# A second load of x in another order of tokens, tiles of neighbouring tokens, and stores per pair of tiles

## The chip, the cores and the metric

One core of a Trainium2 chip runs the kernel. The metric is the device time in microseconds of one execution, as the median of several runs. The engines named below are TensorE (PE; its weight loads are PEld), VectorE (DVE), ScalarE (ACT), GpSimd (POOL) and SyncE (SP); 16 DMA engines move data between HBM and SBUF.

## The reference

x has 4 sequences of 4096 tokens of 512 numbers in float32. Each token is normalised, and two branches are added to it:

```python
xn = _layernorm(x, axis=-1)
x = x + attention(xn) + ffn(xn)

def ffn(xn):                                   # M = 64, INNER = 16
    s = einsum('btd,dm->btm', xn, Win) + bin_
    h = relu(s[..., None] * W1 + b1)           # 16 values for each s
    g = einsum('btmh,mh->btm', h, W2) + b2
    return einsum('btm,md->btd', g, Wout) + bout
```

The attention's result is not zero for the first 16 tokens of a sequence alone (it indexes the token axis with the number of heads), so the kernel computes it once for 64 tokens, beside the main work. Nearly all of the work is the feed-forward branch over 16384 tokens.

## The kernel before

The tokens are taken in 16 **pairs** of blocks, 1024 tokens a pair, 512 a block (`h` or `b`, 0 and 1). A pair of x is 2 MB and lies in one of 6 ring buffers `x_sb`, 128 partitions x 4096 numbers. The kernel is a pipeline of 19 **bodies** (`BODIES = N + 3`): body n loads ahead, transposes pair n and forms s for it, scales and spreads s of pair n-1, takes ReLUs for pairs n-1 and n-2, sums them over the 16 inner values, and projects and adds pair n-3. Every engine has its instructions written out in a fixed order per body (`pe_program`, `act_program`, `dve_program`, `pool_program`, `sp_program`); the attention's instructions are put between them at places of a list (`AT_PE` and the like), up to body 8. Engines meet only by semaphores.

How s gets x with the 512 numbers of a token along the partitions:
- Block 0: PE transposes 128 x 128 pieces of `x_sb` (line 457) into PSUM, ACT copies them to `xT` (line 642).
- Block 1 (from pair 2 on, `n >= BY_PE`): the block is read from HBM **a second time**, into `xq`, such that VectorE's transpose of 32 x 32 squares (line 922) makes the whole turn. Here these are called **quads**. One half of the block, 256 tokens or 0.5 MB, is one `xq` buffer; there are three. Partition group i of 32 holds columns 128 i to 128 i + 127.
- `s_product` (line 478) then multiplies both with the centred Win, block 0 to partitions 0 to 63, block 1 to partitions 64 to 127.

VectorE takes the two transposes of a body (`turn_quads`) at its head and in its middle, between the four additions (`add`, line 912), the statistics of x (line 939), and the product and difference on s. PE's `project` (line 537) loads columns of G as weights and multiplies them with Wout; `add` adds its result to `x_sb` in place, and that is stored. An addition covers one tile of 128 tokens from each of both blocks.

All of these transfers are issued by SP, on one queue. Its order in a body n is: first half of the quads of pair n+1 (8 transfers), first store of pair n-3, both loads of pair n+2, second half of the quads of pair n+1 (8 transfers), second store of pair n-3:

```python
                if n > 2 and has(n + 1):
                    load_quads(2 * (n + 1 - BY_PE))
                if has(n - 3):
                    store(n - 3, 0)
                if n + AHEAD >= RING and has(n + AHEAD):
                    for h in range(2):
                        load(sp, n + AHEAD, h)
                if has(n + 1):
                    load_quads(2 * (n + 1 - BY_PE) + 1)
                if has(n - 3):
                    store(n - 3, 1)
```

A quad half waits until VectorE has turned the half that lay in its buffer, three halves earlier (`tq_done`). A load waits until the stores of the pair that lay in its ring buffer have landed (`st`). A store waits for two of the four additions (`add_done`).

Which token lies where: token p*4 + j of a block lies on partition p, tile j. A partition thus loads 8 KB in one run and stores 4 KB in one run. So that s has the tokens in their own order, PE's transposes write every fourth column of PSUM (`j::TILES`), and `project` reads every fourth column of G. A quad transfer covers 32 neighbouring tokens of all four column groups: 128 rows of 512 bytes, 64 KB.

Of the kernel before, what the change touches and what calls it, by code (L numbers as in the profile page):

```python
# [11 lines left out]
P = 128  # L12
RING = 6
# [7 lines left out]
def residual_block(nc, x, Wq, bq, Wk, Wv, bv, Wo, bo, lna_w, lnc_w, lnd_w, Wlq, blq, Wlk, blk, Wlv, blv,  # L21
# [6 lines left out]
    TPP = 8  # L28
    BLK = TPP // 2 * P
    PAIR = 2 * BLK  # L30
    N = B * T // PAIR
# [12 lines left out]
    NV = 5  # L44
    QH = BLK // QD // 2


    x_v = x.rearrange("b (n h p j) d -> (b n) h p (j d)", h=2, p=P, j=TPP // 2)
    out_v = out.rearrange("b (n h p j) d -> (b n) p h (j d)", h=2, p=P, j=TPP // 2)

    xq_v = x.rearrange("b (n h t a) (i d) -> (b n) h i a t d", h=2, t=BLK // QD, a=QD, d=P)
    pe, act, dve, pool, sp = nc.tensor, nc.scalar, nc.vector, nc.gpsimd, nc.sync
# [4 lines left out]
    with ctx:  # L57
# [14 lines left out]
        xT = sb("xT", [P, DC, BLK])  # L72
        xqT = sb("xqT", [P, BLK // QD, DC, QD])
        xT1 = xqT[:, :, :, :].rearrange("p t c a -> p (t c a)").rearrange("p (c n) -> p c n", c=DC)
        s_full = sb("s_full", [P, BLK])
# [74 lines left out]
        ldq = [sem(f"ldq{r}") for r in range(3)]  # L150
        st = [[sem(f"st{r}{h}") for h in range(2)] for r in range(RING)]
        tr_done, ev_done, tq_done, sc_done = sem("tr_done"), sem("ev_done"), sem("tq_done"), sem("sc_done")
# [61 lines left out]

        def by_part(t, i):

            return t.rearrange("p (h i d) -> p h i d", h=2, d=2 * D)[:, :, i, :]

        def out_part(n, i):
            return out_v[n, :, :, 2 * i * D:2 * (i + 1) * D]  # L220

        HALF = TPP // 2 * D


        def load(queue, n, h):

            m = n % RING
            if n == 3 and h == 0:
                queue.wait_ge(turned, 2 * DC)
            elif n == 4 and h == 0:  # L230
                queue.wait_ge(qk_ps, 1)
            elif n == 5 and h == 0:
                queue.wait_ge(turned, 4 * DC)
            elif n >= RING and h == 0:
                for i in range(2):
                    queue.wait_ge(st[m][i], 16 * (n // RING))
            queue.dma_start(x_sb[m][:, h * HALF:(h + 1) * HALF], x_v[n, h, :, :]).then_inc(ld[m][h], 16)  # L237

        def load_quads(k):

            r, n, h = k % 3, k // 2 + BY_PE, k % 2
            if k > 2:
                sp.wait_ge(tq_done, k - 2)
            for t in range(QH):
                sp.dma_start(xq[r][:, t * P:(t + 1) * P], xq_v[n, 1, :, :, h * QH + t, :]).then_inc(ldq[r], 16)  # L245

        def load_weight(i, w):
            sp.dma_start(w_nat[i], w.rearrange("(c p) i -> p c i", p=P)).then_inc(in_w[i], 16)

        def store(n, i):  # L250
            m = n % RING
            if n < N - 1:
                sp.wait_ge(add_done, TILES * n + 2 * (i + 1))
                sp.dma_start(out_part(n, i), by_part(x_sb[m][:, :], i)).then_inc(st[m][i], 16)  # L254
            else:
                for j in (2 * i, 2 * i + 1):
                    sp.wait_ge(add_done, TILES * n + j + 1)
                    sp.dma_start(out_v[n, :, :, j * D:(j + 1) * D], by_tile(x_sb[m][:, :], j)).then_inc(st[m][i], 16)

        def sp_program():  # L260
# [32 lines left out]
            for n in range(2, BODIES):  # L293
                if n > 2 and has(n + 1):
                    load_quads(2 * (n + 1 - BY_PE))
                if has(n - 3):
                    store(n - 3, 0)
                if n + AHEAD >= RING and has(n + AHEAD):
                    for h in range(2):
                        load(sp, n + AHEAD, h)  # L300
                if has(n + 1):
                    load_quads(2 * (n + 1 - BY_PE) + 1)
                if has(n - 3):
                    store(n - 3, 1)

# [139 lines left out]
        def transpose(n, part):  # L445

            m = n % RING
            for g in (2 * part, 2 * part + 1) if n < BY_PE else (part,):
                b, c = divmod(g, DC)
                if c == 0:  # L450
                    pe.wait_ge(ld[m][b], 16 * (n // RING + 1))
                free = groups(n) + g - (1 if n < BY_PE else 0)
                if free > 0:
                    pe.wait_ge(ev_done, free)
                for j in range(TILES):
                    col0 = b * HALF + j * D + c * P
                    mm = pe.transpose(bank(n, g)[:, j::TILES], x_sb[m][:, col0:col0 + P], ident[:, :])  # L457
                mm.then_inc(tr_done, 1)

        def s_product(n):  # L460
# [9 lines left out]
            for c in range(DC):  # L470
                for b in range(2):
                    if b == 0:
                        w, turned_x = win, xT[:, c, :]
                    elif n < BY_PE:
                        w, turned_x = win, xT1[:, c, :]
                    else:
                        w, turned_x = winq, xqT[:, :, c, :]
                    mm = pe.matmul(s_ps[b * M:(b + 1) * M, :], w[:, c, :], turned_x, start=(c == 0), stop=(c == DC - 1))  # L478
                mm.then_inc(sc_done, 1)

        def spread_rstd(n):
            pe.wait_ge(rstd_done, 2 * n + 2)
            if n > 1:
                pe.wait_ge(g_made, n - 1)
            for j in range(TILES):
                mm = pe.transpose(g_ps[:, j::TILES], rwide[:, j, :, :].rearrange("p b m -> p (b m)"), ident[:, :])
            mm.then_inc(rb_done, 1)
# [36 lines left out]
        def project(n, j):  # L524
# [111 lines left out]
        def evacuate(n, part):  # L636
            for g in (2 * part, 2 * part + 1) if n < BY_PE else (part,):
                b, c = divmod(g, DC)
                act.wait_ge(tr_done, groups(n) + g + 1)
                if n > 0:  # L640
                    act.wait_ge(sc_done, DC * (n - 1) + c + 1)
                act.activation((xT if b == 0 else xT1)[:, c, :], bank(n, g)[:, :], ACT.Copy).then_inc(ev_done, 1)  # L642

# [270 lines left out]
        def turn_quads(n, h):  # L914
# [133 lines left out]
        def pool_program():  # L1048
# [76 lines left out]
            for n in range(0, N, N // B):  # L1125
                for h in range(2):
                    pool.wait_ge(st[n % RING][h], 16 * (n // RING + 1))
            for b in range(B):
# [4 lines left out]
            for m in range(RING):  # L1133
                for h in range(2):
                    pool.wait_ge(st[m][h], 16 * (len(range(m, N, RING)) + (1 if m == (N - 1) % RING else 0)))

# [31 lines left out]
```

## Time and profile before

| | us |
|---|---|
| median of 3 runs | 387.23 (387.21 to 388.0) |
| the profiled execution | 386.97 |
| its span, first to last instruction | 385.2 |
| PE busy | 318.6 (83%) |
| DVE busy | 273.1 (71%) |
| POOL busy | 235.8 (61%) |
| ACT busy | 224.0 (58%) |
| DMA, all queues of SP | 86.93 MB, 63.1% of 16 engines |

Busy time is the share of the span in which an engine had an instruction at work. PE's matmuls are pipelined, so its share says little of how near it is to its peak. The DMA share is the time that packets took, over 16 engines; it says nothing of how evenly these are loaded. SP's instructions here are all issues of DMAs: their durations are the time that the issue took, not the transfer. HBM was read 53.77 MB and written 33.69 MB. The page counts 32 loads of x of 1 MB, 30 stores of 1 MB and 4 of 0.5 MB, and 224 quad transfers of 64 KB.

### The profile page before, as it was taken

The page shows a single profiled execution, that of the slowest core. Times are in us where ns is not written, and L with a number is a line of the kernel's source. Part 1 is how long each engine was busy: PE and PEld are TensorE (multiplying, and loading weights), DVE is VectorE, ACT ScalarE, POOL GpSimd, SP SyncE. Part 2 cuts the span into 40 slices and gives each one's busy share as a digit, 9 for nine tenths or more (in the row PEclk, how much of TensorE's full clock was granted, in tenths as well). Part 3 has the DMA queues.
Part 4 walks back from the last instruction along what each step waited for, and adds up shares of the span by engine and source line. Part 5 has one row for each costly group of instructions (what it writes and reads, how often), then busy time and mean ns, then how long its engine had stood idle before and what let it go on. Part 6 is the DMA issues. An engine that isn't in the chain of part 4 may idle for free.

```text
span 385.2 us, 5266 instructions
## 1 busy us (share of the span) xinstructions
PE 318.6 (83%) x1804; PEld 150.0 (39%) x1804; DVE 273.1 (71%) x422; ACT 224.0 (58%) x278; POOL 235.8 (61%) x209
## 2 busy tenths in 40 slices
PE   4775999788799999997998795949869594899784
PEld 3452554544246344533343242413324241343322
DVE  2779766788898999699983856737395672886534
ACT  1464756437477657575677473735746374578750
POOL 9535938429629693966757390936629093487950
PEclk9998799899699999999999698987969899799999
DMA  8993977644384946557495665848556494462468
GB/s 238 323 406 97 268 238 279 239 172 175 117 287 175 344 172 223 229 208 284 175 322 192 182 244 196 319 173 285 212 186 261 172 339 172 173 260 114 186 154 327
DMA packets 49834, 87.80 MB, mean 228 GB/s; under 512 B 5625, under 2 KB 34449, under 8 KB 45713
## 3 DMA queue, kind: packets, MB, share of 16 engines
q1 hardware_dynamic: 48384, 86.93, 63.1%
q0 software_dynamic: 640, 0.16, 0.7%
q10 hardware_dynamic: 784, 0.39, 0.5%
q8 instruction: 14, 0.23, 0.2%
q14 instruction: 12, 0.09, 0.1%
HBM read 53.77 MB, written 33.69 MB: 227 GB/s over the span
## 4 chain that ended last, share of the span: by engine, by line
SPq 50%; PE 24%; DVE 13%; DMA 5%; issue 5%; ACT 2%; DVEq 0%; ACTq 0%
SPq L245 43%; PE op L537 7%; PE s L478 5%; PE g L515 4%; SPq L237 4%; DVE x L912 3%; DMA x<-in_L_attn_x_dram 3%; SPq L254 3%; DMA xq<-in_L_attn_x_dram 2%; PE T L457 2%; DVE stats L939 2%; DVE w2s L785 2%; PE rep L499 1%; ACT H L667 1%; PE op L340 1%
## 5 line engine op out<-in xcount | busy, mean ns | idle before, releaser
L667 ACT ACTIVATE H<-rep,b1c,w1c 128x1024 f32<-128x1024 f32 x128 | 146.5, 1212 | 53.0 <-PE rep L499 45.5
L1046 POOL TENSOR_TENSOR x<-x,bias_row 128x512 f32<-128x512 f32 x128 | 161.6, 1302 | 5.1 <-DVE bias_row L776 5.1
L912 DVE TENSOR_TENSOR x<-x,op 128x1024 f32<-128x1024 f32 x62 | 75.1, 1212 | 32.9 <-PE op L537 32.9
L1030 POOL TENSOR_TENSOR rstd<-veps,nhalf 128x8 f32<-128x8 f32 x16 | 26.4, 1649 | 104.0 <-DVE veps L949 104.0
L939 DVE BATCH_NORM_STATS2 stats<-x 128x6 f32<-128x512 f32 x128 | 80.7, 679 | 7.8 <-DMA x<-in_L_attn_x_dram 7.6
L537 PE MATMUL op<-wout,G 64*128 64x512 f32 x248 | 81.5, 736 | 5.3 <-DVE x L912 5.3
L922 DVE STREAM_TRANSPOSE xqT<-xq 128x1024 f32<-128x1024 f32 x28 | 34.8, 1241 | 54.7 <-DMA xq<-in_L_attn_x_dram 38.8
L642 ACT ACTIVATE xT<-T 128x512 f32<-128x512 f32 x60 | 36.0, 601 | 50.8 <-PE T L457 50.7
L478 PE MATMUL s<-xT,win 128*64 128x512 f32 x128 | 63.4, 641 | 0.8 <-ACT xqT L642 0.8
L515 PE MATMUL g<-H,w2s 128*32 128x512 f32 x512 | 63.7, 607 | 0.4 <-ACT H L667 0.4
L478 PE MATMUL s<-xqT,winq 128*64 128x512 f32 x112 | 56.2, 648 | 0.0
L457 PE MATMUL T<-ident,x 128*128 128x128 f32 x256 | 43.2, 293 | 5.5 <-DMA x<-in_L_attn_x_dram 3.4
L499 PE MATMUL rep<-SH,spread 64*128 64x512 f32 x64 | 21.7, 673 | 30.3 <-DVE SL L933 29.2
L457 PEld LDWEIGHTS T<-ident,x 128*128 128x128 f32 x256 | 29.0, 147 | 39.7 <-issue 32.6
L537 PEld LDWEIGHTS op<-wout,G 64*128 64x128 f32 x248 | 34.6, 316 | 21.1 <-issue 13.2
L478 PEld LDWEIGHTS s<-xT,win 128*64 128x64 f32 x128 | 17.6, 149 | 45.9 <-issue 45.9
L515 PEld LDWEIGHTS g<-H,w2s 128*32 128x32 f32 x512 | 12.8, 109 | 35.6 <-issue 25.7
L499 PEld LDWEIGHTS rep<-SH,spread 64*128 64x128 f32 x64 | 6.6, 200 | 36.9 <-DVE SL L933 31.7
L1032 POOL TENSOR_TENSOR rwide<-rstd,ones_d 128x512 f32<-128x512 f32 x16 | 17.9, 1118 | 1.3
L478 PEld LDWEIGHTS s<-xqT,winq 128*64 128x64 f32 x112 | 15.5, 151 | 0.0
L340 PE MATMUL op<-ident,x 128*128 128x128 f32 x64 | 10.5, 316 | 4.9 <-DVE x L794 4.9
L499 PE MATMUL rep<-SL,spread 64*128 64x512 f32 x64 | 14.4, 444 | 0.0
(170 smaller groups left out, 301.7 us busy)
## 6 DMA issues: line engine op xcount, KB each, us to landing
x<-in_L_attn_x_dram SPq DMA_DIRECT2D x32, 1024.0 KB, 9.9
out_dram<-x SPq DMA_DIRECT2D x30, 1024.0 KB, 6.2
xq<-in_L_attn_x_dram SPq DMA_DIRECT2D x224, 64.0 KB
out_dram<-x SPq DMA_DIRECT2D x4, 512.0 KB, 3.2
x<-in_L_attn_Wq_dram SPq DMA_DIRECT2D x1, 1024.0 KB, 17.5
x<-in_L_attn_Wk_dram SPq DMA_DIRECT2D x1, 1024.0 KB, 19.6
x<-in_L_attn_Wv_dram SPq DMA_DIRECT2D x1, 1024.0 KB, 7.6
x<-in_L_attn_Wo_dram SPq DMA_DIRECT2D x1, 1024.0 KB, 10.2
```

Of the source, the lines that this page charges most:

```text
L245: sp.dma_start(xq[r][:, t * P:(t + 1) * P], xq_v[n, 1, :, :, h * QH + t, :]).then_inc(ldq[r], 16)
L457: mm = pe.transpose(bank(n, g)[:, j::TILES], x_sb[m][:, col0:col0 + P], ident[:, :])
L478: mm = pe.matmul(s_ps[b * M:(b + 1) * M, :], w[:, c, :], turned_x, start=(c == 0), stop=(c == DC - 1))
L499: mm = pe.matmul(rep_ps[:, b * BLK:(b + 1) * BLK], spread[own, half, :], part[own, :], start=(part is SH), stop=(part is SL), tile_positio ...
L515: mm = pe.matmul(g_ps[at0:at0 + MH, :], w2s[:, half, k, :], Hr[half][k % len(Hr[half])][:, b * BLK:(b + 1) * BLK], start=(k == 0), stop=(k ...
L537: mm = pe.matmul(sum_banks(n, j)[:, b * D:(b + 1) * D], G[n % 2][own, j::TILES], wout[own, :], start=True, stop=True, tile_position=(b * M ...
L642: act.activation((xT if b == 0 else xT1)[:, c, :], bank(n, g)[:, :], ACT.Copy).then_inc(ev_done, 1)
L667: act.activation(Hr[half][k % len(Hr[half])][:, :], rep_ps[:, :], ACT.Relu, bias=b1c[:, half, k:k + 1], scale=w1c[:, half, k:k + 1]).then_ ...
L912: dve.tensor_tensor(both, both, sum_banks(n, j)[:, :].rearrange("p (h d) -> p h d", h=2), ALU.add).then_inc(add_done, 1)
L922: dve.transpose(xqT[:, h * QH:(h + 1) * QH, :, :].rearrange("p t c a -> p (t c a)"), xq[k % 3][:, :]).then_inc(tq_done, 1)
L939: dve.bn_stats(stats[:, j, :], x_sb[m][:, j * D:(j + 1) * D]).then_inc(bn_done, 1)
L1046: pool.tensor_tensor(x_sb[m][:, c], x_sb[m][:, c], bias_row[:, :], ALU.add).then_inc(xc_done, 1)
```

## The change

A token's place changes: token j*128 + p of a block lies on partition p, tile j. A load brings four runs of 2 KB to each partition; PE's transposes write 128 neighbouring columns of PSUM, and `project` reads 128 neighbouring columns of G. `out_v` is written tile by tile: four stores of 0.5 MB a pair, each after its own addition, in runs of 2 KB, under one semaphore a ring buffer. A quad half becomes one transfer of 0.5 MB: 256 neighbouring tokens of all four column groups, 1024 rows of 512 bytes, of which eight neighbouring tokens go to each partition. VectorE's transpose then writes with a step of eight elements, so that `xqT` has the tokens in order, and `s_product` reads it without a step. SP's order becomes: both halves of the quads of pair n+1, both loads of pair n+2, the four stores of pair n-3. The final waits of POOL follow the new counts.

```diff
+    QH = BLK // QD // 2
-    x_v = x.rearrange("b (n h p j) d -> (b n) h p (j d)", h=2, p=P, j=TPP // 2)
-    out_v = out.rearrange("b (n h p j) d -> (b n) p h (j d)", h=2, p=P, j=TPP // 2)
-    xq_v = x.rearrange("b (n h t a) (i d) -> (b n) h i a t d", h=2, t=BLK // QD, a=QD, d=P)
+    x_v = x.rearrange("b (n h j p) d -> (b n) h p j d", h=2, p=P, j=TPP // 2)
+    out_v = out.rearrange("b (n h j p) d -> (b n) j p h d", h=2, p=P, j=TPP // 2)
+    xq_v = x.rearrange("b (n u k) (i d) -> (b n) u i k d", u=4, k=QD * QH, d=P)
...
-        xqT = sb("xqT", [P, BLK // QD, DC, QD])
+        xqT = sb("xqT", [P, DC, BLK])
...
-                for i in range(2):
-                    queue.wait_ge(st[m][i], 16 * (n // RING))
-            queue.dma_start(x_sb[m][:, h * HALF:(h + 1) * HALF], x_v[n, h, :, :]).then_inc(ld[m][h], 16)
+                queue.wait_ge(st[m], 16 * TILES * (n // RING))
+            queue.dma_start(x_sb[m][:, h * HALF:(h + 1) * HALF].rearrange("p (j d) -> p j d", d=D), x_v[n, h, :, :, :]).then_inc(ld[m][h], 16)
...
-            for t in range(QH):
-                sp.dma_start(xq[r][:, t * P:(t + 1) * P], xq_v[n, 1, :, :, h * QH + t, :]).then_inc(ldq[r], 16)
+            sp.dma_start(xq[r][:, :], xq_v[n, 2 + h, :, :, :]).then_inc(ldq[r], 16)
...
-        def store(n, i):
+        def store(n, j):
             m = n % RING
-            if n < N - 1:
-                sp.wait_ge(add_done, TILES * n + 2 * (i + 1))
-                sp.dma_start(out_part(n, i), by_part(x_sb[m][:, :], i)).then_inc(st[m][i], 16)
-            else:
-                for j in (2 * i, 2 * i + 1):
-                    sp.wait_ge(add_done, TILES * n + j + 1)
-                    sp.dma_start(out_v[n, :, :, j * D:(j + 1) * D], by_tile(x_sb[m][:, :], j)).then_inc(st[m][i], 16)
+            sp.wait_ge(add_done, TILES * n + j + 1)
+            sp.dma_start(out_v[n, j, :, :, :], by_tile(x_sb[m][:, :], j)).then_inc(st[m], 16)
...
             for n in range(2, BODIES):
-                if n > 2 and has(n + 1):
-                    load_quads(2 * (n + 1 - BY_PE))
-                if has(n - 3):
-                    store(n - 3, 0)
+                if has(n + 1):
+                    if n > 2:
+                        load_quads(2 * (n + 1 - BY_PE))
+                    load_quads(2 * (n + 1 - BY_PE) + 1)
                 if n + AHEAD >= RING and has(n + AHEAD):
                     for h in range(2):
                         load(sp, n + AHEAD, h)
-                if has(n + 1):
-                    load_quads(2 * (n + 1 - BY_PE) + 1)
                 if has(n - 3):
-                    store(n - 3, 1)
+                    for j in range(TILES):
+                        store(n - 3, j)
...
-                    mm = pe.transpose(bank(n, g)[:, j::TILES], x_sb[m][:, col0:col0 + P], ident[:, :])
+                    mm = pe.transpose(bank(n, g)[:, j * P:(j + 1) * P], x_sb[m][:, col0:col0 + P], ident[:, :])
...
-                        w, turned_x = winq, xqT[:, :, c, :]
+                        w, turned_x = winq, xqT[:, c, :]
...
-                mm = pe.matmul(sum_banks(n, j)[:, b * D:(b + 1) * D], G[n % 2][own, j::TILES], wout[own, :],
+                mm = pe.matmul(sum_banks(n, j)[:, b * D:(b + 1) * D], G[n % 2][own, j * P:(j + 1) * P], wout[own, :],
...
-            dve.wait_ge(ldq[k % 3], 16 * QH * (k // 3 + 1))
+            dve.wait_ge(ldq[k % 3], 16 * (k // 3 + 1))
...
-            dve.transpose(xqT[:, h * QH:(h + 1) * QH, :, :].rearrange("p t c a -> p (t c a)"), xq[k % 3][:, :]).then_inc(tq_done, 1)
+            dve.transpose(xqT[:, :, h * QH * QD:(h + 1) * QH * QD].rearrange("p c (a t) -> p t c a", t=QH), xq[k % 3][:, :].rearrange("p (t c b) -> p t c b", t=QH, b=QD)).then_inc(tq_done, 1)
```

The transposes that spread the factors of the norm (`spread_rstd`) change from `j::TILES` to `j * P:(j + 1) * P` in the same way.

## Rows read from the trace of the kernel before

**Rows 1.** The page, part 4: the chain that ended last, shares of the span.
```profile
SPq L245 43%; PE op L537 7%; PE s L478 5%; PE g L515 4%; SPq L237 4%; DVE x L912 3%; DMA x<-in_L_attn_x_dram 3%; SPq L254 3%; DMA xq<-in_L_attn_x_dram 2%; PE T L457 2%; DVE stats L939 2%; DVE w2s L785 2%; PE rep L499 1%; ACT H L667 1%; PE op L340 1%
```

**Rows 2.** Waits of VectorE, 155 to 343 us: who <- whom: us, times, longest.
```profile
DVE xqT L922 <- DMA xq<-in_L_attn_x_dram: 37.0, 8, 7.2
```

**Rows 3.** SP's timeline over one pair: start, duration, line, transfer, count.
```profile
218.70 11.58 SPq L245 DMA_DIRECT2D xq<-in_L_attn_x_dram  x8
230.33 0.65 SPq L254 DMA_DIRECT2D out_dram<-x  x1
231.02 7.78 SPq L245 DMA_DIRECT2D xq<-in_L_attn_x_dram  x8
238.85 0.66 SPq L254 DMA_DIRECT2D out_dram<-x  x1
239.61 1.43 SPq L237 DMA_DIRECT2D x<-in_L_attn_x_dram  x2
```

**Rows 4.** Line 245 alone: issue durations, ns min/median/max.
```profile
L245 SPq DMA_DIRECT2D xq<-in_L_attn_x_dram x224: 543/694/6672, 17.3 to 338.2; - x112
```

**Rows 5.** Windows: engines' busy us (count), granted clock, DMA share, GB/s.
```profile
227.60:231.00 3.40, 3.40 (x28) 1.50 (x28) 1.14 (x2) 3.40 (x5) 3.27 (x3) 1.00 0.29 86
231.60:233.00 1.40, 1.34 (x12) 0.42 (x4) 0.00 (x0) 0.03 (x1) 0.00 (x0) 1.00 1.04 391
234.20:235.40 1.20, 0.00 (x0) 0.00 (x0) 1.20 (x2) 0.00 (x0) 0.00 (x0) 1.00 0.27 109
242.40:244.00 1.60, 1.60 (x10) 0.50 (x7) 0.55 (x2) 0.30 (x1) 1.60 (x2) 1.00 1.01 248
244.40:248.60 4.20, 4.20 (x25) 2.46 (x28) 2.90 (x4) 3.07 (x5) 4.20 (x5) 1.00 1.00 422
```

**Rows 6.** SP's timeline about 100 us and before the last quads.
```profile
91.41 7.79 SPq L245 DMA_DIRECT2D xq<-in_L_attn_x_dram  x8
103.64 0.38 SPq L254 DMA_DIRECT2D out_dram<-x  x1
...
334.76 4.14 SPq L245 DMA_DIRECT2D xq<-in_L_attn_x_dram  x4
```

**Rows 7.** Windows about 103 us and behind SP's last quad issue.
```profile
102.30:104.30 2.00, 2.00 (x11) 0.34 (x10) 1.91 (x3) 0.02 (x1) 2.00 (x3) 0.55 0.02 6
...
339.10:340.10 1.00, 1.00 (x4) 0.41 (x4) 0.32 (x1) 1.00 (x3) 1.00 (x2) 1.00 0.29 86
```

**Rows 8.** VectorE's timeline: a sum, the next pair's transpose, the last transpose.
```profile
240.51 1.22 DVE L912 TENSOR_TENSOR x<-x,op 128x1024 f32<-128x1024 f32 x1
243.97 1.25 DVE L922 STREAM_TRANSPOSE xqT<-xq 128x1024 f32<-128x1024 f32 x1 [1.05 <-PE s L478]
...
342.65 1.25 DVE L922 STREAM_TRANSPOSE xqT<-xq 128x1024 f32<-128x1024 f32 x1 [0.57 <-DMA xq<-in_L_attn_x_dram]
```

**Rows 9.** Windows of seven pairs, from transpose to transpose: the first, and the sum.
```profile
165.60:188.70 23.10, 19.53 (x129) 8.86 (x125) 22.28 (x32) 16.15 (x21) 16.53 (x14) 1.00 0.64 230
...
sum 160.00, PE 130.18 PEld 54.86 DVE 105.89 ACT 95.29 POOL 93.97; mean PE 18.60 PEld 7.84 DVE 15.13 ACT 13.61 POOL 13.42
```

**Rows 10.** Windows of 2 KB weight rows, 4 KB stores, 2 KB stores.
```profile
19.00:23.00 4.00, 3.13 (x24) 2.13 (x20) 1.54 (x4) 1.67 (x4) 0.68 (x2) 1.00 1.05 384
...
376.50:378.00 1.50, 1.04 (x7) 0.33 (x4) 1.43 (x2) 0.00 (x0) 0.00 (x0) 1.00 1.02 407
...
379.00:384.00 5.00, 1.23 (x6) 0.52 (x4) 2.35 (x2) 0.00 (x0) 0.00 (x0) 1.00 1.02 380
```

**Rows 11.** Weight loads by line (537 of G, 382 of qT's block): ns min/median/max.
```profile
L537 PEld LDWEIGHTS op<-wout,G x248: 304/326/333, 65.5 to 378.1; 64*128 64x128 f32 x124
...
L382 PEld LDWEIGHTS A<-qT,bd x6: 186/189/192, 76.1 to 150.7; 128*128 128x128 f32 x6
```

**Rows 12.** The chain behind 342 us: project, first and last of nine.
```profile
346.95 0.86 PE op L537 x4
...
379.10 1.15 PE rep L537 x4
```

More of the change, by code:

```diff
@@ L44, in residual_block @@
     NV = 5
-    QH = BLK // QD // 2
-    x_v = x.rearrange("b (n h p j) d -> (b n) h p (j d)", h=2, p=P, j=TPP // 2)
-    out_v = out.rearrange("b (n h p j) d -> (b n) p h (j d)", h=2, p=P, j=TPP // 2)
-    xq_v = x.rearrange("b (n h t a) (i d) -> (b n) h i a t d", h=2, t=BLK // QD, a=QD, d=P)
+    x_v = x.rearrange("b (n h j p) d -> (b n) h p j d", h=2, p=P, j=TPP // 2)
+    out_v = out.rearrange("b (n h j p) d -> (b n) j p h d", h=2, p=P, j=TPP // 2)
+    xq_v = x.rearrange("b (n u k) (i d) -> (b n) u i k d", u=4, k=QD * QH, d=P)
     pe, act, dve, pool, sp = nc.tensor, nc.scalar, nc.vector, nc.gpsimd, nc.sync
@@ L72, in residual_block @@
         xT = sb("xT", [P, DC, BLK])
-        xqT = sb("xqT", [P, BLK // QD, DC, QD])
-        xT1 = xqT[:, :, :, :].rearrange("p t c a -> p (t c a)").rearrange("p (c n) -> p c n", c=DC)
+        xqT = sb("xqT", [P, DC, BLK])
         s_full = sb("s_full", [P, BLK])
@@ L150, in residual_block @@
         ldq = [sem(f"ldq{r}") for r in range(3)]
-        st = [[sem(f"st{r}{h}") for h in range(2)] for r in range(RING)]
+        st = [sem(f"st{r}") for r in range(RING)]
         tr_done, ev_done, tq_done, sc_done = sem("tr_done"), sem("ev_done"), sem("tq_done"), sem("sc_done")
@@ L213, in by_tile @@
             return t.rearrange("p (h j d) -> p h j d", h=2, d=D)[:, :, j, :]
[L215 to L220, printed above, removed]
         HALF = TPP // 2 * D
@@ L474, in s_product @@
                     elif n < BY_PE:
-                        w, turned_x = win, xT1[:, c, :]
+                        w, turned_x = win, xqT[:, c, :]
                     else:
-                        w, turned_x = winq, xqT[:, :, c, :]
+                        w, turned_x = winq, xqT[:, c, :]
                     mm = pe.matmul(s_ps[b * M:(b + 1) * M, :], w[:, c, :], turned_x, start=(c == 0), stop=(c == DC - 1))
@@ L485, in spread_rstd @@
             for j in range(TILES):
-                mm = pe.transpose(g_ps[:, j::TILES], rwide[:, j, :, :].rearrange("p b m -> p (b m)"), ident[:, :])
+                mm = pe.transpose(g_ps[:, j * P:(j + 1) * P], rwide[:, j, :, :].rearrange("p b m -> p (b m)"), ident[:, :])
             mm.then_inc(rb_done, 1)
@@ L641, in evacuate @@
                     act.wait_ge(sc_done, DC * (n - 1) + c + 1)
-                act.activation((xT if b == 0 else xT1)[:, c, :], bank(n, g)[:, :], ACT.Copy).then_inc(ev_done, 1)
+                act.activation((xT if b == 0 else xqT)[:, c, :], bank(n, g)[:, :], ACT.Copy).then_inc(ev_done, 1)
         def copy_rstd(n):
@@ L1125, in pool_program @@
             for n in range(0, N, N // B):
-                for h in range(2):
-                    pool.wait_ge(st[n % RING][h], 16 * (n // RING + 1))
+                pool.wait_ge(st[n % RING], 16 * TILES * (n // RING + 1))
             for b in range(B):
@@ L1133, in pool_program @@
             for m in range(RING):
-                for h in range(2):
-                    pool.wait_ge(st[m][h], 16 * (len(range(m, N, RING)) + (1 if m == (N - 1) % RING else 0)))
+                pool.wait_ge(st[m], 16 * TILES * len(range(m, N, RING)))
         sp_program()
```

## The prediction

> **What bounds the kernel now.** I read the chain of waits first. SP's issue of the second copy of x (the "quads", line 245) carries 43% of it [rows 1]. That invites the reading "SP can't issue fast enough", so next I looked at who waits for it: from 155 to 343 us VectorE's transpose of the quads waits 8 times for a quad transfer, 37.0 us in all, 4.6 us a body [rows 2]. Compute is faster than what feeds it.
>
> Then the question is whether SP or the transfers are slow. In SP's timeline one pair takes 20 issues [rows 3]: eight quad issues in 11.58 us, a store, eight in 7.78 us, a store, two loads. Issues of the same form last 0.54 us at the least and 6.67 us at the most [rows 4]: the long ones are SP waiting for room. The windows say for what [rows 5]. While only quads flow (227.6 to 231.0) the DMA share is 0.29 of 16 engines at 86 GB/s: the work of four engines and a little overlap. A store then fills all 16 (1.04), and when twelve are through with it a share of 0.27 at 109 GB/s is left for over a microsecond: four engines have their part of the store still to do, because they were busy with quads. So it is the same four each time. At the end, after SP's last quad issue is over (334.76 + 4.14 = 338.9), 339.1 to 340.1 still shows 86 GB/s, and VectorE waits for the last half until 342.65 [rows 6 to 8]. So SP is held up by four engines, and not they by SP.
>
> What four engines do for a pair, by the same windows: quads, 1.05 MB at 86 GB/s, 12.2 us; their quarter of two 1 MB stores, 0.52 MB at 109 GB/s, 4.8 us; their quarter of the 2.1 MB load, 0.52 MB at 422/4 = 105.5 GB/s [rows 5], 5.0 us. Sum 22.0 us. A body (the work between two such transposes, one pair) lasts 160.0/7 = 22.9 us [rows 9]. Of the 0.9 us left, 0.64 is the stretch in which a store meets the load behind it: all engines taken (1.01) and only 248 GB/s from 242.4 to 244.0, 1.6 x (1 - 248/415), 415 being the mean of the load's 422 and a store's 407 [rows 5, 10]. The four engines are thus full, and the kernel is bound by them. The one hole I find after the start is 102.3 to 104.3, share 0.02 [rows 7]: SP had issued its quads by 99.2 and waited until 103.6 to store [rows 6].
>
> The Trainium skill has this rule too (DMA: Bandwidth & Descriptors, section on why a DMA increments its semaphore by 16): a transfer is spread over the largest number up to 16 that divides the slowest dimension of both sides. The quads' source has 4 column blocks outermost, so 4; the trace agrees, with 0.29 and 86 GB/s.
>
> **The change, part by part.**
> *Quads in two transfers.* 16 issues become 2. The outermost dimension of the source stays 4 and the runs stay 512 bytes, so I take four engines and 12.2 us a pair as before. Bounds: if each piece of 64 KB cost the engines something outside its rows, the gain is at most what a body leaves unexplained, 0.9 - 0.64 = 0.26 us, for 14 pairs 3.6 us; on the other side rival 4. I take 0, since 86 GB/s holds over stretches of several pieces. SP's saved time is hidden: it waits for the engines anyway. [...]
>
> *Loads in runs of 2 KB instead of 8 KB.* Weights come in 2 KB runs: 384 GB/s on all engines (19 to 23 us) against 422 for x [rows 5, 10]. Quarter of a pair: 0.524 MB/96 = 5.46 against 4.97, +0.49 us. All 16 pairs' loads lie ahead of the last quads: +7.8 us. The lower bound is 0; I take the row.
>
> *Stores in runs of 2 KB, four a pair.* The last pair already does it: 380 GB/s against 407 for 4 KB runs [rows 10]; 4.8 x (407/380 - 1) = +0.34 us a pair. Stores of 11 pairs lie ahead of the last quads: +3.7 us, lower bound 0. The Trainium skill speaks against both edits (Perfetto Trace Analysis, DMA Optimizations: raise transfers from 2 KB to 4 or 8 KB); by the rows it is 6 to 9%, and nothing in my sum comes from the page.
>
> *Order on SP's queue.* Before: quads, store, load, quads, store. After: both quads, load, four stores. Each edit's waits:
> - The second half's wait is for the transpose of the first half of the body, which comes at the head of VectorE's body; SP reaches it after 6 us of the first half's flow. No hole.
> - The load's wait is for all four stores of pair n-4, the last issued before 12 us of quads: hidden.
> - The fourth store waits for a sum late in the body. Behind it stand the next quads, on which VectorE and then PE depend. Ahead of it are 12.2 + 5.5 + 3.9 = 21.6 us of work for the four engines, and the sums come a body (22.9 us) apart, and 3.5 us ahead of the next body's transpose (240.51, 243.97) [rows 8]. While the queue lags, as it does now, it never runs dry. If that cover were gone, each body would show a hole of one to two us.
> - The hole at 102.3 goes: behind the first half now comes the second, which waits for no sum: -2.0 us (bounds 0 and -2.0).
> - Half of a pair's stores (the one that VectorE's first two sums release) moves behind the last quads: 0.26 MB/109 = -2.4 us.
> - Store-before-load meets 10 times (pairs 6 to 15). Now the stores come behind the load. The slow mix may go (-0.64 x 10 = -6.4) or stay (0); nothing in the trace shows that order. I take the middle, -3.2.
> VectorE now waits at the first half and no longer at the second; it is the same wait at another place.
>
> *Token order.* TensorE's transposes write PSUM without a step of four, s reads the turned quads without one: 0, hidden like all of PE's work by VectorE's 4.6 us of waiting in a body; behind the last quads 8 such transposes and one s are left, so even 10% of them would be under half a microsecond. Weight loads from G lose their step of four: 326 ns, against 189 ns for a contiguous one [rows 11]. Up to 342 us this hides behind the DMA. Behind it, project lies on the chain about 9 times [rows 12]; the first of its two weight loads is exposed: 9 x 0.137 = -1.2 us (bounds 0, and -2.4 if both are). VectorE's transpose writes with a step of 8 elements; no row shows it. With the ratio 326/189 it would be 1.25 -> 2.15 us; below, it is 1.25. I take 1.25; one lies on the final chain (0 to +0.9), the others in the body's 4.6 us of waiting.
>
> **Sum.** Last quads: +7.8 + 3.7 - 2.0 - 2.4 - 3.2 = +3.9 us. Behind them the same 42.5 us of compute, less 1.2. Total +2.7 on the profiled execution's 386.97 us (span 385.2 and 1.8 around it), which is 0.3 below the median of 387.23: **389.7 us**. Bounds together: with costly mix, hole kept and slow transpose 7.8 + 3.7 - 2.4 + 0.9 = +10.0, 397; with runs of 2 KB free, -2.0 - 2.4 - 6.4 - 2.4 = -13.2, 374. The likeliest's own range is 388.1 to 394.
>
> **Rivals.**
> 1. *Not slower: the order is worth more than the run length.* Place: the four engines' queue between 150 and 342 us. For it: the lower rates for 2 KB are read with all 16 engines in flow, while four alone reach 27.3 GB/s each with 4 KB (109/4) against 25.4 (407/16) [rows 5, 10]; and the slow mix was seen only where a load comes behind a store. Against: 27.3 against 25.4 says nothing of 2 KB, and a load still stands beside stores. With half of the run cost (+5.8) and the whole mix gone: 5.8 - 2.0 - 2.4 - 6.4 - 1.2 = -6.2, 381 us. It decides from where the runs cost less than 5.6 us plus what the mix gives back. Chance 0.30: half of that within 0.2%, near the deciding point, half below, around 381.
> 2. *SP, or a fixed cost a transfer, is the bound.* For it: 43% of the chain; a median issue of 0.69 us is also 64 KB at some 90 GB/s [rows 4]. Against: quads flow after the last issue [rows 6, 7], and four engines lag in stores [rows 5]. VectorE's 37.0 us of waiting would go: 387 - 37 = 350 us. Chance 0.05.
> 3. *The two transfers spread over 16 engines,* so that the change does more than it says. Quads then take 12.2/4 = 3 us a pair and again the 37 us go: 350 us. Against: the 4 is still outermost. Chance 0.03.
> 4. *A transfer of 1024 rows doesn't fit the queue.* From the last issue's end to VectorE's start the queue held 3.75 us of quads [rows 6, 8], some 600 rows. Were the rows of a transfer that is longer than this served engine after engine, each half would take about 12 us instead of 6: 14 x 12 = +168, 558 us. Nothing shows it. Chance 0.04.
>
> **How the numbers follow.** Forecast 0.58 (all of it slower). Within 0.2% (0.8 us, about what a measurement can tell here): half of rival 1, 0.15. Faster: its other half, and rivals 2 and 3: 0.23. Slower: 0.58 + rival 4 = 0.62. Range 378 to 397 us: it takes in rival 1 and the upper bound and leaves out rivals 2 to 4 and the edges, under 2 in 10.
>
> **What would show it.** Right: quad-only stretches still 0.27 to 0.29 at 86 GB/s; bodies of 23.1 to 23.8 us; VectorE's wait for quads at the first half of each pair; the stretch at 102 us without a hole; two issues of about 6 us each on SP, blocked; weight loads from G near 190 ns. Wrong: quad-only stretches above 100 GB/s (rival 3, or 2), a body under 22.9 us (rival 1), holes of DMA share near 0 in every body (SP waiting for the fourth sum), a quad half over 7 us (rival 4), or VectorE's transpose at 2 us.

## The result, and the profile after

| | before | after |
|---|---|---|
| median, us | 387.62 (387.21 to 388.28) | 407.25 (403.23 to 414.0, 4 runs) |
| profiled execution, its span | 386.97, 385.2 | 403.23, 401.5 |
| DVE busy | 273.1 | 292.4 |
| DMA packets | 49834 | 69496 |

The ratio is 1.047 (1.039 to 1.055): 5% slower, some 18 us, and outside the range that I gave. The profiled execution stands at 403.23, 4 us under the median. Medians are of all runs, but ratios, here and below, leave out single slow executions (here the 414.0).

The chain of the changed kernel (the page, part 4) no longer hangs on SP's issues, as in [rows 1]: waiting for a long transfer is now booked on the transfer itself.
```profile
DMA xq<-in_L_attn_x_dram 30%; DVE x L897 8%; PE op L522 8%; PE s L463 5%; DVE xqT L907 4%; DVE stats L924 4%; POOL x L1031 4%; SPq L228 3%; DMA x<-in_L_attn_x_dram 3%; PE g L500 2%; DVE w2s L770 2%; PE T L442 1%; SPq L244 1%; PE rep L484 1%
```
VectorE's wait for quads from 155 to 358 us, against [rows 2] (first line), and all of SP's waits for VectorE (the two below):
```profile
DVE xqT L907 <- DMA xq<-in_L_attn_x_dram: 39.1, 7, 8.3
...
SPq L244 <- DVE x L897: 53.3, 28, 6.3
SPq L235 <- DVE xqT L907: 40.0, 14, 10.8
```
The last line had no counterpart before: SP waits 14 times for a transpose before it may issue quads. What this costs is taken up under b_order. SP over one pair, against [rows 3] (line 235 quads, 228 loads, 244 stores):
```profile
237.04 13.78 SPq L235 DMA_DIRECT2D xq<-in_L_attn_x_dram  x2
250.86 6.69 SPq L228 DMA_DIRECT2D x<-in_L_attn_x_dram  x2
257.60 3.72 SPq L244 DMA_DIRECT2D out_dram<-x  x4
261.36 13.14 SPq L235 DMA_DIRECT2D xq<-in_L_attn_x_dram  x2
```
Such a cycle lasts 261.36 - 237.04 = 24.3 us. The windows that answer [rows 5] (busy us and count by engine, granted clock, DMA share, GB/s): first three stretches of quads alone, then the place where load and stores meet, then stores.
```profile
223.00:226.00 3.00, 3.00 (x18) 1.06 (x16) 2.94 (x8) 3.00 (x5) 0.00 (x0) 1.00 0.29 87
...
247.50:251.00 3.50, 2.16 (x16) 1.24 (x12) 0.00 (x0) 2.57 (x5) 3.50 (x4) 1.00 0.29 86
251.00:256.00 5.00, 0.00 (x0) 0.00 (x0) 2.11 (x2) 2.05 (x2) 5.00 (x5) 0.86 0.26 74
...
259.00:263.00 4.00, 4.00 (x22) 1.28 (x24) 3.83 (x4) 1.94 (x3) 0.00 (x0) 0.70 1.04 342
264.00:268.00 4.00, 4.00 (x30) 1.55 (x24) 3.97 (x10) 1.82 (x3) 0.00 (x0) 1.00 1.05 406
```
Two of the stretches are what I forecast, 0.29 and 86 to 87 GB/s. The third is not: for 5 us the share is 0.26 and 74 GB/s flow. Part of that is the lower share: the four engines are not all at work all the time. The start of the kernel shows something else, where the first two long transfers run by themselves: there the share is full (0.30) and the rate is still only 72.
```profile
34.00:36.00 2.00, 2.00 (x12) 0.51 (x8) 2.00 (x3) 2.00 (x3) 2.00 (x3) 1.00 0.30 72
```
The same two us of the kernel before, with its pieces of 64 KB:
```profile
34.00:36.00 2.00, 0.00 (x0) 0.00 (x0) 2.00 (x7) 0.00 (x0) 0.00 (x0) 0.96 0.29 87
```
VectorE's transposes (start, duration), against [rows 8]: the second half of pair 8, a first half of a steady pair, the first half and the second of the last pair.
```profile
200.31 2.07 DVE L907 STREAM_TRANSPOSE xqT<-xq 128x1024 f32<-128x1024 f32 x1
...
253.89 2.05 DVE L907 STREAM_TRANSPOSE xqT<-xq 128x1024 f32<-128x1024 f32 x1 [7.67 <-DMA xq<-in_L_attn_x_dram]
...
350.46 2.05 DVE L907 STREAM_TRANSPOSE xqT<-xq 128x1024 f32<-128x1024 f32 x1 [6.98 <-DMA xq<-in_L_attn_x_dram]
...
357.48 2.05 DVE L907 STREAM_TRANSPOSE xqT<-xq 128x1024 f32<-128x1024 f32 x1
```
A pair takes (350.46 - 253.89)/4 = 24.1 us. Weight loads from G, against [rows 11] (the group's busy us and mean ns stand behind the bar):
```profile
L522 PEld LDWEIGHTS op<-wout,G 64*128 64x128 f32 x248 | 21.6, 205 | 61.3 <-DVE x L897 46.5 <-issue 13.9
```

**Where the time went.** One table serves for all kernels below. It is read from VectorE's timeline: when the transpose of pair 8's second half starts (until there compute is the slower side), when the last one does (between them the transfers are), and the end of the span. The last column is the mean rate of the DMA engines from pair 8 to the last half. The table holds for one execution each: those of b_quads and a_half2 are the fastest of their kernels, 4.4 and 5.0 us under the medians.

| kernel | pair 8 | last half | end | after pair 8 | behind last | GB/s |
|---|---|---|---|---|---|---|
| before | 188.7 | 342.6 | 385.2 | 153.9 | 42.6 | 225 |
| after | 200.3 | 357.5 | 401.5 | 157.2 | 44.0 | 214 |
| b_order | 186.9 | 351.5 | 397.8 | 164.6 | 46.3 | 217 |
| b_order2 | 188.1 | 346.3 | 392.3 | 158.2 | 46.0 | 224 |
| a_oldquads | 187.0 | 351.9 | 396.0 | 164.9 | 44.1 | 213 |
| b_quads | 195.7 | 351.7 | 395.7 | 156.0 | 44.0 | 222 |
| b_strided | 193.8 | 345.4 | 388.6 | 151.6 | 43.2 | 227 |
| b_flat2 | 190.3 | 345.4 | 387.8 | 155.1 | 42.4 | 224 |
| b_load2k | 193.5 | 350.1 | 392.9 | 156.6 | 42.8 | 222 |
| b_store4 | 187.9 | 339.7 | 381.9 | 151.8 | 42.2 | 227 |
| a_half2 | 196.0 | 349.2 | 393.7 | 153.2 | 44.5 | 219 |
| a_flat | 194.5 | 360.8 | 404.8 | 166.3 | 44.0 | 205 |

Of the changed kernel's +16.3 us, 11.6 are there by pair 8, 3.3 come after it and 1.4 behind the last quads, where I had -1.2. Two rows split the 11.6: a_flat, without the slow transpose, is 5.8 late at pair 8, and a_half2, with transfers half as long, 7.3. After pair 8 the changed kernel moves 33.6 MB (157.2 us at 214 GB/s), the kernel before 34.6 MB (153.9 us at 225): 5% less rate, and 1 MB less left to move.

### The profile page after: what moved, and what is told of

Same layout as the page of the kernel before. It is cut to its first block, busy times and chain, and to the rows that moved or that the text cites. A ratio compares the mean times of both kernels' runs of the same rounds, so it can differ in the third digit from the quotient of the medians.

```text
span 401.5 us, 5085 instructions
## 1 busy us (share of the span) xinstructions
PE 317.4 (79%) x1804; PEld 137.9 (34%) x1804; DVE 292.4 (73%) x422; ACT 224.7 (56%) x278; POOL 235.4 (59%) x209
## 2 busy tenths in 40 slices
DMA packets 69496, 87.79 MB, mean 219 GB/s; under 512 B 5320, under 2 KB 34144, under 8 KB 69472
## 4 chain that ended last, share of the span: by engine, by line
DMA 32%; DVE 26%; PE 23%; issue 6%; POOL 5%; SPq 5%; ACT 2%; DVEq 0%; POOLq 0%; ACTq 0%
DMA xq<-in_L_attn_x_dram 30%; DVE x L897 8%; PE op L522 8%; PE s L463 5%; DVE xqT L907 4%; DVE stats L924 4%; POOL x L1031 4%; SPq L228 3%; DMA x<-in_L_attn_x_dram 3%; PE g L500 2%; DVE w2s L770 2%; PE T L442 1%; SPq L244 1%; PE rep L484 1%; DVE WvT L849 1%
## 5 line engine op out<-in xcount | busy, mean ns | idle before, releaser
L522 PE MATMUL op<-wout,G 64*128 64x512 f32 x248 | 77.5, 705 | 44.7 <-DVE x L897 44.7
L907 DVE STREAM_TRANSPOSE xqT<-xq 128x1024 f32<-128x1024 f32 x28 | 58.1, 2076 | 46.8 <-DMA xq<-in_L_attn_x_dram 40.7
L500 PE MATMUL g<-H,w2s 128*32 128x512 f32 x512 | 67.3, 637 | 0.0
L463 PE MATMUL s<-xT,win 128*64 128x512 f32 x128 | 60.7, 619 | 0.8 <-ACT xqT L627 0.8
L463 PE MATMUL s<-xqT,winq 128*64 128x512 f32 x112 | 51.2, 599 | 0.0
L442 PE MATMUL T<-ident,x 128*128 128x128 f32 x256 | 45.6, 305 | 5.8 <-DMA x<-in_L_attn_x_dram 3.9
L442 PEld LDWEIGHTS T<-ident,x 128*128 128x128 f32 x256 | 30.5, 153 | 43.3 <-issue 35.1
L522 PEld LDWEIGHTS op<-wout,G 64*128 64x128 f32 x248 | 21.6, 205 | 61.3 <-DVE x L897 46.5
L500 PEld LDWEIGHTS g<-H,w2s 128*32 128x32 f32 x512 | 13.0, 111 | 42.6 <-issue 29.9
L912 DVE TENSOR_TENSOR s_full<-s,s_full 128x512 f32<-128x512 f32 x16 | 10.9, 683 | 6.8 <-ACT s_full L633 6.8
L1006 POOL TENSOR_TENSOR rstd<-var,nhalf 128x16 f32<-128x16 f32 x3 | 8.8, 2919 | 9.7 <-ACT var L603 9.7
```

What stands on the lines that cost most here:

```text
L442: mm = pe.transpose(bank(n, g)[:, j * P:(j + 1) * P], x_sb[m][:, col0:col0 + P], ident[:, :])
L500: mm = pe.matmul(g_ps[at0:at0 + MH, :], w2s[:, half, k, :], Hr[half][k % len(Hr[half])][:, b * BLK:(b + 1) * BLK], start=(k == 0), stop=(k ...
L907: dve.transpose(xqT[:, :, h * QH * QD:(h + 1) * QH * QD].rearrange("p c (a t) -> p t c a", t=QH), xq[k % 3][:, :].rearrange("p (t c b) -> ...
```

## The experiments

Times are medians; each ratio is to the kernel before, run beside it. Code is cut to the lines that matter.

**b_quads: the kernel before with the quads' edit alone.**
```diff
-            for t in range(QH):
-                sp.dma_start(xq[r][:, t * P:(t + 1) * P], xq_v[n, 1, :, :, h * QH + t, :])
+            sp.dma_start(xq[r][:, :], xq_v[n, 2 + h, :, :, :])      # and the transpose with a step of 8
```


> The kernel before with the quads' part of the change alone: two transfers a pair in place of 16, and VectorE's transpose writing with a step of eight; rows, stores and SP's order stay. Theory A (the four engines' queue is the bound, and the change lost its time by shorter rows and by the mix of loads and stores): 388 to 390 us, quad-only stretches at 86 GB/s. Theory B (one long quad transfer and the slower transpose, 2.08 us in place of 1.25, are the loss): at least half of the 16 us, 395 us or more, with holes in the DMA share near quads.


Measured: 401.96 us, ratio 1.034 (1.027 to 1.041). The edit that I had put at nothing costs 13 us by the ratio. Theory B, but the holes that it expected are not there: its only one is 1 us at 106 us, where the kernel before has 2.

**b_order: only SP's new order.** In a scheme, for one body:
```diff
-  quads 0 | store 0 | both loads | quads 1 | store 1
+  quads 0 | quads 1 | both loads | store 0 | store 1
```


> The kernel before with SP's new order alone: both quad halves, both loads, two stores. Theory A: the hole at 102 us goes (-2.0), 0.5 MB of stores moves behind the last quads (-2.4), the meeting of load and store stays or goes (0 to -6.4): 377 to 384 us. Theory C (the order itself is the loss, because loads and stores stand together and slow each other on all 16 engines): 388 to 395 us.


Measured: 398.73 us, 1.029 (1.022 to 1.035); beyond the dearest of the theories. Its windows: in the steady part the quads flow below 86 GB/s here too, with short pieces, and the loads meet stores for 3 us at 262. The last line is SP's wait for transposes in the whole kernel.
```profile
244.00:249.00 5.00, 0.13 (x2) 0.00 (x0) 0.79 (x1) 3.52 (x5) 5.00 (x5) 0.90 0.26 79
...
256.00:259.00 3.00, 3.00 (x28) 0.68 (x24) 2.53 (x5) 0.86 (x2) 0.00 (x0) 1.00 0.92 262
...
SPq L245 <- DVE xqT L921: 0.5, 1, 0.5
```
SP waits 0.5 us for transposes here, against 40.0 in the changed kernel. So that wait does not come from the order alone: it is 2.1 us with half as long transfers (a_half2) and 43.6 with the long ones and a fast transpose (a_flat). The 11 us that b_order loses are not in it, and what it costs in the changed kernel, if anything, no run shows.

**a_oldquads: the changed kernel with the quads' part undone.**


> The changed kernel with the quads as before: 16 transfers a pair, transpose without a step. Theory A: still slow, 402 to 407 us. Theory B: it gains at least half of the 16 us, below 397 us.


Measured: 396.44 us, 1.023 (1.019 to 1.028). Theory B, if only just. By the ratios, order, rows, stores and token order together cost 9 us, the quads' part another 9. Its time is not above b_order's, though it has the loads' rows of 2 KB as well. Behind the last quads it takes 44.1 us, b_order 46.3: that fits the contiguous weight loads (-1.2, bounds 0 and -2.4), but the four stores are in it too, and the token order was not run alone.

**b_quadsflat and b_strided: the quads' edit cut in two.** The first has the long transfer and a contiguous transpose, the second short transfers and the transpose with a step of 8. Both leave the tokens of each second block out of order.


> The kernel before with the quads in one transfer for each half, but VectorE's transpose writes contiguously as before, so that the tokens of each pair's second block stand in another order in s (the output is then not the reference's). It cuts b_quads' +14 us in two. Theory L (the long transfer costs: SP is held for a whole half, the next half or the store starts ragged or late): 398 to 402 us, as b_quads, and SP's issues of the quads stay at 12 us or more a body. Theory T (the transpose at 2.08 us costs: each half is released 0.83 us later, and SP waits for it before it can issue the next one): 387 to 391 us. Both in part: 391 to 398.

> The kernel before with its 16 quad transfers a pair, but VectorE's transpose of the quads writes with a step of 8 elements, as in the changed kernel (tokens of each second block are permuted in s; the output is not the reference's). Theory L: the transposes' 2.08 us hide in VectorE's 4.6 us of waiting in a body: 387 to 389 us. Theory T: the late release of the quads' buffers is paid in each half, 14 x 0.83 = +11.6: 396 to 401 us. In each case the transpose should last 2.05 to 2.1 us.


Measured: b_strided 389.99 us, 1.0065 (1.0045 to 1.0084), transposes of 2.08 us:
```profile
L923 DVE STREAM_TRANSPOSE xqT<-xq 128x1024 f32<-128x1024 f32 x28 | 58.3, 2084 | 43.8 <-DMA xq<-in_L_attn_x_dram 28.5 <-PE s L479 15.3
```
The transpose alone costs 2.5 us: it is 5.1 us late at pair 8, where VectorE has little to wait for, and the transfers win 2.3 of them back. b_quadsflat took 394.1 us once and about 404 three times, so that no ratio can be given; even the fastest is 6.7 us above the kernel before, more than the transpose costs. Theory L, but with a size that this pair leaves wide.

**b_flat2: each half in two transfers of 512 rows.**


> The kernel before with each half of the quads in two transfers of 512 rows, between the 8 of 128 rows (387.4 us) and the one of 1024 rows (394 to 405 us with the same contiguous transpose); tokens of each second block stand in another order in s. Theory R (the cost grows with the rows of a transfer: in the long one the quad stretch runs below 86 GB/s at its start, and the four engines end apart): 390 to 398 us, and the stretch from 31 to 39 us, where only quads flow, at 75 to 85 GB/s. Theory O (it is the order of tokens, 8 neighbours behind each other into one partition, not the size): 398 us or more. Theory S (it is SP, which is only held one transfer long and reaches its waits elsewhere): 385 to 390.


Measured: 389.86 us, 1.0054 (1.0024 to 1.0083), and the early stretch at full rate:
```profile
34.00:36.00 2.00, 1.03 (x6) 0.14 (x2) 2.00 (x3) 2.00 (x2) 2.00 (x3) 1.00 0.29 87
```
Half the rows cost 2 us and no rate. Theory O is out. Theory R asked for 75 to 85 GB/s, and its time is just missed; the time is at the edge of theory S, which this run does not exclude. The larger loss comes between 512 and 1024 rows, not in proportion. One thing changes along with the length: a partition gets 1 token from a transfer of 128 rows, 4 neighbouring ones from 512 rows and 8 from 1024. No run has one without the other.

**b_load2k and b_store4: the rows alone.**
b_store4 writes each store of 1 MB as two of 512 KB. The edit of b_load2k:
```diff
-            queue.dma_start(x_sb[m][:, h * HALF:(h + 1) * HALF], x_v[n, h, :, :]).then_inc(ld[m][h], 16)
+            queue.dma_start(x_sb[m][:, h * HALF:(h + 1) * HALF], x_v[n, h, :, :], max_dma_last_dim=2048).then_inc(ld[m][h], 16)
```


> The kernel before with nothing changed but the rows of x's loads: at most 2 KB each, as in the changed kernel. My sum's term: +0.49 us a pair for the four engines, +7.8 us, so 395 us (392 to 397). Rival, rows of 2 KB cost nothing when four engines are the bound (their packets follow each other as fast as long ones): 386.5 to 389.

> The kernel before with each store of 1 MB in two of 512 KB with rows of 2 KB, issued in the same two places of SP's order. My sum's term: +0.34 us a pair for the four engines on 11 pairs, +3.7 us, so 391 us (389.5 to 393). Rival, free: 386.5 to 388.5.


Measured: b_load2k 393.71 us, 1.015 (1.010 to 1.021), near the +7.8 of the sum. b_store4 385.47 us, 0.995 (0.992 to 0.998): the four stores of 2 KB rows cost nothing and gain 2 us, where I had +3.7.

**b_order2: as b_order, but the load behind the stores.**


> The kernel before with both halves of the quads one behind the other, then both stores, then the load: it differs from b_order (398.7 us, bodies of 24.1 us) only in that the load stands behind the stores, as before. Theory M (in b_order the load, met from behind by stores, is what costs): bodies of 22.6 to 23 us and 384 to 390 us. Theory H (two halves without a store between them cost, because VectorE and the sums wait in one piece): bodies of 24 us, 395 to 400 us.


Measured: 394.01 us, 1.015 (1.010 to 1.020). Between the theories: of b_order's 11 us this takes 4.7 away. Its windows at the same place of a pair:
```profile
244.00:249.00 5.00, 0.56 (x6) 0.32 (x3) 1.83 (x2) 3.95 (x5) 5.00 (x5) 1.00 0.29 86
...
255.00:258.00 3.00, 3.00 (x20) 0.61 (x22) 1.62 (x2) 0.82 (x2) 0.00 (x0) 0.85 0.96 266
```
The quads are back at 0.29 and 86. The slow meeting of load and stores is not gone: 3 us at 266 GB/s here, 3 us at 262 in b_order, 1.6 us at 248 in the kernel before [rows 5], where one store instead of two meets the load. By the measure of the prediction, 1.6 x (1 - 248/415) = 0.64 us in that body of the kernel before, 3 x (1 - 262/415) = 1.1 in this one of b_order. That is one body each. Summed by the same measure over every microsecond between pair 8 and the last half with a share over 0.9 and less than 350 GB/s, the loss is 4.8 us before, 3.5 in b_order, 4.5 in b_order2 and 5.3 in the changed kernel. So the order changed the mix little, and the difference between b_order and b_order2 is not in it. It is in the quads: of the microseconds with a share of at most 0.36, 16 of 78 run below 80 GB/s in b_order, 2 of 79 in b_order2 and 5 of 72 before. That the stores right ahead of the quads leave the four engines apart would explain it, but is not shown.

**a_half2 and a_flat: what costs in the changed kernel itself.** a_half2 has two transfers of 512 rows a half, a_flat the long ones with a contiguous transpose (and each second block's tokens out of order).


> The changed kernel (407 us) with each half of the quads in two transfers of 512 rows instead of one of 1024; VectorE's transpose then writes with a step of 4 elements instead of 8. Theory R (in the changed kernel too the row count of the transfer costs: slow start, engines apart): 394 to 399 us, near the 396.4 of the changed kernel with 16 short transfers. Theory X (the transfers' size costs only in the old order of SP's queue, and what is left over in the changed kernel is the slow transpose): 402 to 408 us.

> The changed kernel (407 us) with its two long transfers a pair, but with a transpose that writes contiguously, 1.25 us instead of 2.08 (tokens of each second block stand in another order in s). Theory R: the transposes cost 2.5 us, as in b_strided, 403 to 406 us. Theory X: the transposes are what costs in the changed kernel, 395 to 399 us.


Measured: a_half2 400.44 us, 1.027 (1.019 to 1.035), with transposes of 2.09 us; a_flat 406.22, 1.046 (1.043 to 1.050). Taking away the transfers' length gives 7 us back, near theory R, taking away the slow transpose 1 us, within what the changed kernel's own runs differ. That 1 us is a difference of two larger ones: a_flat is 5.8 us earlier at pair 8 and takes 9.1 longer after it, with 30 of its 83 quad-only microseconds below 80 GB/s against 12 of 75 in the changed kernel and 5 of 71 in a_half2. Why there are more of them in a_flat is open.

**b_q16: the quads on 16 engines.** Each half in four transfers, one a block of 128 columns; the outermost dimension is then 32, not 4. It has 8 issues a pair, more than the changed kernel's 2 and fewer than 16.
```diff
+            for i in range(DC):
+                sp.dma_start(xq[r][i * QD:(i + 1) * QD, :].rearrange("p (t d) -> p t d", d=P), xq_v[n, 1, i, :, h * QH:(h + 1) * QH, :])
```


> The kernel before with the quads of a half in four transfers, one a block of 128 columns, whose outermost dimension is 32 on both sides in place of 4 and 128; everything else as before. If four engines are the bound, and the outermost dimension sets their number, quads no longer take 12.2 us a pair of four engines but some 3 us of all: no stretch at 86 GB/s, VectorE's 37 us of waiting for quads goes, 345 to 360 us. If the number of engines is not set by that dimension, 387 us. If SP's issues were the bound: 8 issues a pair in place of 16, also about 350 us, but then quad-only stretches stay at 86 GB/s.


Measured: 344.32 us, 0.887 (0.881 to 0.893), just under the range. A window in which quads flow (a store is issued 0.3 us into it), and then the chain:
```profile
220.20:221.80 1.60, 1.60 (x8) 0.89 (x8) 1.60 (x3) 1.60 (x3) 1.60 (x2) 1.00 1.23 252
```
```profile
PE 66%; DVE 23%; issue 4%; DMA 3%; ACT 2%; SPq 0%; DVEq 0%; ACTq 0%
```
All engines carry quads: of 290 half microseconds from 155 to 300 us, one still shows four engines at 80 to 92 GB/s, of 374 before (155 to 342) 135 do. The 252 GB/s may hold some of the store. VectorE no longer waits for a transfer of quads, and TensorE leads the chain.

**a_q16, q16_order, a_best: the change's parts where no four engines are full.** a_q16 is the changed kernel with that split; q16_order is b_q16 with SP's new order; a_best is the changed kernel with that split and the kernel before's layout of the quads, so that the transpose is contiguous.


> The changed kernel with each half of the quads in four transfers, one a block of 128 columns, as in b_q16 (344.3 us), so that no four engines carry them alone. Theory: the changed kernel's losses in the quads (slow start, engines apart) go with the long transfer, and VectorE becomes the bound: 344.3 plus 20 to 28 transposes that are 0.83 us longer, 360 to 370 us. Rival 1: the order of SP's queue or the 2 KB rows still bind: 375 to 395 us. Rival 2: the transposes hide: 343 to 350 us.

> b_q16 (344.3 us) with SP's new order (both halves, both loads, two stores), the same edit that cost +11 us in the kernel before. Theory F (the order costs because four engines are full and lie apart, and nobody waits for them any more): 342 to 347 us. Theory H (it costs because stores come late and VectorE's transposes wait in one piece): 352 to 358 us.

> The changed kernel's tokens, rows, stores and order of the queue, with the quads as before (contiguous transpose) but each half in four transfers, one a block of 128 columns, so that 16 engines carry them. Against a_q16 (354.4 us) it takes 0.83 us off each of VectorE's 28 transposes, against q16_order (341.8 us) it has TensorE's contiguous loads of G. If VectorE's transposes are what bound a_q16, 332 to 341 us; if the 2 KB rows or PE bind, 341 to 350 us.


Measured: a_q16 354.39 us, 0.915 (0.909 to 0.921); q16_order 341.78, 0.880 (0.875 to 0.885); a_best 340.85, 0.879 (0.873 to 0.885). The order that cost 11 us costs nothing here, as theory F had it. The 2 KB rows cost nothing that a_best's contiguous weight loads don't make up for. a_q16 is faster than its 360 to 370 and still 13.5 us above a_best, which differs in the transpose and in which tokens a transfer brings side by side. VectorE leads a_q16's chain, so the transpose is the likely cause:
```profile
DVE 49%; PE 24%; issue 12%; POOL 8%; DMA 3%; ACT 2%; SPq 0%; DVEq 0%; POOLq 0%; ACTq 0%
```
a_best and q16_order can't be told apart; both beat the kernel before by 12%.

## Why the prediction was wrong

*Right.* The bound was read rightly: b_q16 takes the four engines out of it and 43 us with it. The direction, the price of the loads' rows alone (+7.8 forecast, +6 measured), the four engines for a quad transfer and the contiguous loads of G (205 ns for 316 in the mean) held as well. So did three signs: the hole at 102 us is gone, SP is held about 6.9 us by each quad transfer (13.78 for two), and VectorE's five long waits for quads, 7 to 8.3 us, are all for first halves. In the changed kernel as a whole the rows' price does not show: a_oldquads has them and is no slower than b_order. The one sign of being wrong that came is VectorE's transpose at 2 us.

*Wrong, step 1: "Quads in two transfers ... I take 0".* I argued from a rate that held over several pieces and looked for a cost of pieces; I never asked for a cost of length beyond rival 4's extreme. The transfer of 1024 rows flows at 72 GB/s for part of its time where pieces flow at 87, and a_half2 shows what length costs in the changed kernel, 7 us. In the kernel before (b_quads) the whole edit comes to 13, of which the transpose alone explains 2.5. My bound, 0 below and +168 above, had no weight between: rival 4 was all or nothing. Why a long transfer flows slower at a full share isn't shown, nor whether it is its length or the 8 neighbouring tokens that each partition gets.

*Wrong, step 2: "it is the same wait at another place".* The order was to gain 7.6 us (-2.0 - 2.4 - 3.2), and b_order alone loses 11. "No hole" itself held: from 60 us to the last half no half microsecond of b_order or of the changed kernel has a share under 0.12. SP's wait for transposes doesn't explain the loss either, as above.

4.7 us are the load ahead of the stores (b_order against b_order2), with quads at 79 GB/s instead of 86. The rest, b_order2's 6.3 us, stands in the table (one execution, 7.1) as +4.3 after pair 8 and +3.4 behind the last quads, less 0.6 early. The 4.3 are not a lower rate: b_order2 runs at 224 GB/s there against 225. But it moves 35.4 MB there against 34.6, because by pair 8 it had moved 42.7 MB against 44.3. With the new order the transfers get less far ahead while compute bounds.

The 3.4 are an error of their own: I kept "the same 42.5 us of compute". Behind the last transpose VectorE has 14 additions in both kernels. But in b_order2 it stood still for 6.6 us until the last pair's first half came, at 339.99, and starts the last half 6.3 us later without a wait for it. The addition behind that waits 1.4 us for TensorE, where it waited for nothing before. So the last arrival that holds up compute is the first half, and more work than I counted comes after it. What holds TensorE there isn't shown.

*Wrong, step 3: the mix, "I take the middle, -3.2".* It did not go. Summed over the stretch it is 3.5 to 5.3 us in the three kernels with the new order and 4.8 before, so about 0 where I had -3.2. In the changed kernel the place is less deep and longer, 342 GB/s for 4 us, and its 2 KB loads count in it.

*Wrong, step 4: the transpose at 1.25 us.* It is 2.08, near what the ratio of strided to contiguous weight loads had suggested (2.15), and it was hidden only after pair 8. The 4.6 us of waiting a body were read where the transfers bind; from 60 to 195 us VectorE waits 2.1 us for quads in all, and b_strided is 5.1 us late at pair 8.

*Wrong, a size: the stores,* +3.7 forecast, -2 measured.

**Why the parts don't add up.** Alone they make 11 + 6 + 13 - 2 = 28 us, together 18. The table points at the reason: b_order loses nothing before pair 8 and 10.7 us after it, b_quads 7.0 before and 2.1 after, and the changed kernel 11.6 before and only 3.3 after. A delay in the stretch that compute bounds gives the transfers time to run ahead, and this pays for part of what they lose later. By pair 8 the changed kernel has moved 44.7 MB, b_order 42.4 and a_oldquads 42.8, at mean rates of 223 to 229 GB/s. Single times for the parts can't be added for this reason. That it accounts for all of the 10 us is not shown.

The Trainium skill advises to coalesce many small transfers into one large one, and says that under 64 KB one pays mostly overhead (DMA: Bandwidth & Descriptors, Rules for kernel authors). The pieces here are 64 KB, at that limit, and the trace does not agree with the advice for them: the kernel with 16 such pieces a pair beats the one with 2 transfers (387.56 against 401.96 us, b_quads). The Trainium skill's rule on the slowest dimension (DMA: Bandwidth & Descriptors, Why a DMA increments its semaphore by 16 and not by 1) is what b_q16 used, and the trace agrees: stretches at 86 GB/s became one at 252.

## What to carry to other kernels

When a few DMA engines are full, first ask which dimension spreads the transfer, and change that; the size and order of transfers were worth 5% here, the split by column block 11%. Cost an edit in each stretch of the kernel by that stretch's bound: waiting that hides it in one half need not exist in the other. When bounds lie far apart (0 and +168), put something between them.

## What the runs showed of the hardware that I had not expected

- A transfer of 1024 rows of 512 bytes on four engines, with 8 neighbouring tokens to a partition, runs at 72 GB/s for part of its time, at an unchanged share of busy time (0.30); in two of 512 rows, with 4 to a partition, it runs at 87 (34 to 36 us, the changed kernel and b_flat2).
- The place where loads and stores meet moves 248 to 266 GB/s at a share of 0.92 to 1.01, whichever comes first (kernel before, b_order, b_order2); in the changed kernel, with loads and stores in rows of 2 KB, 342.
- VectorE's transpose of 128 x 1024 fp32 takes 1.24 us if it writes contiguously, 2.08 with a step of 8 elements and 2.09 with a step of 4.
- Stores with rows of 2 KB in pieces of 512 KB are no slower than those of 4 KB in 1 MB (0.995).
